# First block of an attention stage: where TensorE computes absorbed weights, biases, value tiles and the folded projection

## Chip, cores and metric

One core of one Trainium2 chip runs one program. The metric is device microseconds (us) of one execution, lower is better; the kernel before has a median of 724.17 us over 3 runs (723.96 to 729.38).

## What is computed

Two transformer layers over x of 2048 x 128 fp32, each an attention and a mixture of experts, with a layer norm before each of the four. Only the first attention matters here (8 heads, head width 128, latent width 32):

```
c_q = h @ W_DQ + b_DQ;  c_kv = h @ W_DKV + b_DKV          # h = layernorm(x), 2048 x 32 each
q = [c_q @ W_UQ + b_UQ, c_q @ W_QR + b_QR]                 # per head: 128 + 32
k = [c_kv @ W_UK + b_UK, h @ W_KR + b_KR]                  # the last 32 are shared by the heads
attn = softmax(q @ k.T / sqrt(160))
o = attn @ (c_kv @ W_UV + b_UV)
x = x + o @ W_O + b_O
```

## The kernel before

**Absorbed form.** For each head, W_UQ and W_UK (with the W_QR part) are multiplied once into a 128 x 128 matrix, the absorbed weights; with it the latents of the whole sequence (`kk`, 2048 columns) become this head's keys in latent space (`key`). Scores are then products of latent queries with `key`. The value side stays latent too (`val`, 2048 x 32): W_UV and W_O are multiplied into one matrix a head (`proj`, the folded projection), and the biases of value and output give one row (`g_b`), which is spread over 128 partitions (`g_bias`) and added to X. Heads come in two groups of four: group 0 is `absorbed(0)`, group 1 `absorbed(1)`.

**Blocks.** A block n is one head and 512 queries; there are 32. For each block TensorE makes two things. *Row products* (`rows`, `half_rows`, L1507): 128 queries against 1024 keys as two halves of 512 columns in two PSUM banks; eight of them, called chunks, make a block, and VectorE takes the maximum of each (`chunk_max`, L1087 for both halves in one instruction ahead of the first block, L1093 for one half within the blocks), then the negative maximum of all queries (`minus_max`, L1101, tile `nmx`), which SyncE's DMA puts into `q_cols` as one more row (the shift). *Scores* (`scores`, L1521): 128 keys against 512 queries, which ScalarE turns into exponentials (L651), sixteen tiles a block, in three PSUM banks (0, 1, 2). The exponentials go into the weighted sums (`weighted`, L1565, eight tiles a call). Row products run ten chunks (LEAD) ahead of the scores, so chunks 0 to 9 are made before the first block: chunks 0 to 7 belong to block 0, 8 and 9 to block 1.

**Order of the work.** Each engine has one instruction list written by hand, and semaphores between them. A block's loop has eight slots; in each TensorE makes two score tiles and the two halves of one row product. A table worked out ahead (`BANK`, `BEFORE`) gives the items of the loop the banks 3 to 6 in turn, in the order in which they are listed, and `bank_read` waits until the item that was in the bank has been read. `chunks_read(c)` waits until VectorE has read chunks 0 to c - 1.

**What stands around the change.** Ahead of the first block TensorE alternates row products with the rest of the preparation: `absorbed(1)` into bank 2 (L1470, L1471, four heads), `key_biases(1, 1)` (L1476) and the row `g_bias` (L1666) into bank 1, `queries(1, 0)` (L1461) into bank 0, and value tiles (`values`, L1464) into bank 7. Each has a reader: ScalarE and then VectorE split absorbed weights into a high and a low part (L605, L1072), VectorE reads the key biases (L1116, L1119), ScalarE copies `g_bias` (L675), and ScalarE and VectorE make `q_rows` of the query product (L600, L1066). A row product of the first chunk of a block uses that block's `q_rows`: for chunk 8 it is the query block 1. In `half_rows` this stands as

```
if h == 0 and c == 0 and j == 0:
    pe.wait_ge(s_cq, k + 1)
```

Behind chunk 9 TensorE waits for all of these readers at once before the first score tile. In the first block value tiles 12 to 15 stand in slot 1, VectorE's addition of the value bias (L1123) in slot 2, and `folded()` (L1482, 32 matmuls of the code into two banks) in slot 5, with ScalarE's two copies of it (L610) ahead of exponential 12. `weighted(0, 0)` stands in slot 6.

Of the kernel before, what the change touches and what calls it, by code (L numbers as in the profile page):

```python
# [14 lines left out]
TPB = BLK // P  # L15
# [3 lines left out]
def build_kernel(nc, d, out):  # L19

    S, D = d["L0_attn_h_t"].shape[1:]
    NT = S // P
# [10 lines left out]
    with ctx:  # L33
# [213 lines left out]
        for n in range(NBLK):  # L247
            todo = []
            for slot in range(CPB):
                for lin in row_pairs(n, slot):  # L250
                    todo += [("rows", 2 * lin), ("rows", 2 * lin + 1)]
                todo += [("keys", e) for e in key_parts(n, slot)]
                if slot == 0 and n < 2:
                    todo.append(("queries", n + 2))
                if slot == 5 and n == 0:
                    todo += [("folded", 0), ("folded", 1)]
                if slot == 1 and 4 <= n < NBLK - 2:
                    todo.append(("out", n - 4))
                if (slot == 6 and n == NBLK - 3) or (slot == 3 and n == NBLK - 2):
                    todo.append(("out", n - 3))  # L260
                if slot == 1 and n == NBLK - 2:
                    todo.append(("sums", n - 2))
                if slot == 6 and 2 <= n < NBLK - 2:
                    todo.append(("sums", n - 2))
                if slot == 6 and n == NBLK - 2:
                    todo.append(("out", n - 2))
            for item in todo:
                place_item(item, 3 + turn % 4)
                turn += 1
# [177 lines left out]
        with nc.Block() as block:  # L447
# [104 lines left out]
            def _(act):  # L552
# [50 lines left out]
                def absorbed_hi(m):  # L603
                    act.wait_ge(s_a_ps, m + 1)
                    act.copy(wa_hi[:, 4 * m:4 * (m + 1), :], ps[:, A_BANK[m], :].rearrange("p (h c) -> p h c", h=4)).then_inc(s_wah, 1)  # L605
# [67 lines left out]
                keys_hi(3, 0)  # L673
                act.wait_ge(s_b_ps, 2)
                act.copy(g_bias[:, :], ps[:, 1, 0:D]).then_inc(s_gbias, 1)  # L675
                absorbed_hi(1)
                queries_hi(1, 0)
                for n in range(NBLK):
                    for t in range(NT):
                        if t == 4 and n >= 1:  # L680
                            sums(n - 1)
                        if t == (14 if n < NBLK - 2 else 4) and n >= 2:
                            sums_out(n - 2)
                        if t == 10 and n == NBLK - 1:
                            sums_out(n - 1)
                        if t % 2 == 0 and t >= 2:
                            for e in key_parts(n, t // 2 - 1):
                                keys_hi(e, BANK["keys", e])
                        if t == 2 and n < 2:
                            queries_hi(n + 2, BANK["queries", n + 2])  # L690
                        if t == 12 and n == 0:
                            folded()
                        exponential(n, t)
                        if n == NBLK - 1 and t == 10:
                            ln0_act(act, 0, 3)
# [347 lines left out]
            def _(dve):  # L1043
# [135 lines left out]
                        dve.tensor_tensor(g_b[:, :], ps[0:1, 1, 0:D], b_o[:, :], ALU.add).then_inc(s_gb, 1)  # L1179
                minus_max(0)  # L1180
                queries_lo(1, 0)
                absorbed_lo(1)
                key_biases(1, 1)
                for lin in range(CPB, LEAD):
                    chunk_max(lin)
                for n in range(NBLK):
                    for slot in range(CPB):
                        lins = row_pairs(n, slot)
# [251 lines left out]
            def _(pe):  # L1440
# [23 lines left out]
                    return pe.matmul(ps[:, U, t * C:(t + 1) * C], hT[:, t // TPB, t % TPB * P:(t % TPB + 1) * P], w_kk[:, 0:C],  # L1464
                                     start=True, stop=True)

                def absorbed(m):
                    for h in range(4 * m, 4 * (m + 1)):
                        o = ps[:, A_BANK[m], (h % 4) * P:(h % 4 + 1) * P]
                        pe.matmul(o, ukT[:, h, :], uqT[:, h, :], start=True, stop=False)  # L1470
                        last = pe.matmul(o, qr_at[:, h, :], place[:, :], start=False, stop=True)  # L1471
                    last.then_inc(s_a_ps, 1)

                def key_biases(m, bank):
                    for h in range(4 * m, 4 * (m + 1)):
# [38 lines left out]
                def scores(n, t):  # L1514

                    g = NT * n + t
                    if t == 0:
                        pe.wait_ge(s_shift, 16 * (n + 1))
                    if g >= 3:
                        pe.wait_ge(s_exp, g - 2)  # L1520
                    pe.matmul(ps[:, g % 3, :], key[:, n // NB % KBUF, t * P:(t + 1) * P], q_cols[:, n % NB, :],  # L1521
                              start=True, stop=True).then_inc(s_sc, 1)

# [133 lines left out]
                rows(4)  # L1657
                chunks_read(4)
                rows(5)
                absorbed(1)  # L1660
                chunks_read(5)
                rows(6)
                pe.wait_ge(s_gb, 1)
                key_biases(1, 1)
                pe.wait_ge(s_const, N_ONES)
                pe.matmul(ps[:, 1, 0:D], ones_row[:, :], g_b[:, :], start=True, stop=True).then_inc(s_b_ps, 1)  # L1666
                chunks_read(6)
                rows(7)
                queries(1, 0)
                for t in range(2 * TPB):  # L1670
                    values(t)
                chunks_read(7)
                rows(8)
                chunks_read(8)
                rows(9)
                for t in range(2 * TPB, 3 * TPB):
                    values(t)
                pe.wait_ge(s_kb, 3)
                pe.wait_ge(s_gbias, 1)
                pe.wait_ge(s_cq, 2)  # L1680
                pe.wait_ge(s_wal, 2)
                for n in range(NBLK):
                    for slot in range(CPB):
                        scores(n, 2 * slot)
                        for lin in row_pairs(n, slot):
                            bank_read(("rows", 2 * lin))
                            half_rows(lin, 0)
                        scores(n, 2 * slot + 1)
                        for lin in row_pairs(n, slot):
                            bank_read(("rows", 2 * lin + 1))  # L1690
                            half_rows(lin, 1)
                        for e in key_parts(n, slot):
                            bank_read(("keys", e))
                            keys(e, BANK["keys", e])
                        if slot == 0 and n < 2:
                            bank_read(("queries", n + 2))
                            queries(n + 2, BANK["queries", n + 2])
                        if slot == 1 and n == 0:
                            for t in range(3 * TPB, NT):
                                last = values(t)  # L1700
                            last.then_inc(s_val_ps, 1)
                        if slot == 5 and n == 0:
                            bank_read(("folded", 0))
                            bank_read(("folded", 1))
                            folded()
                        if slot == 1 and 4 <= n < NBLK - 2:
                            output(n - 4)
                        if (slot == 6 and n == NBLK - 3) or (slot == 3 and n == NBLK - 2):
                            output(n - 3)
                        if slot == 6 and n == NBLK - 2:  # L1710
                            output(n - 2)
                        if slot == 6:
                            weighted(n, 0)
                        if slot == 6 and 2 <= n < NBLK - 2:
                            totals(n - 2)
                        if slot == 6 and n == NBLK - 1:
                            last_totals(0)
                            last_totals(1)
                        if slot == 1 and n >= 1:
                            weighted(n - 1, 1)  # L1720
                        if slot == 1 and n >= NBLK - 2:
                            totals(n - 2)
                        if n == NBLK - 1:
                            if slot == 2:
                                output(n - 2)
                            elif slot == 4:
                                totals(n - 1)
                                bank_read(("norm", 0))
                                ln0_pe(pe, 0, 3)
                            elif slot == 7:  # L1730
                                output(n - 1)
                                last_totals(2)
                                bank_read(("norm", 1))
                                ln0_pe(pe, 1, 4)
                                weigh(n, range(2 * NG, 3 * NG))
# [350 lines left out]
```

## Time and profile before

| | |
|---|---|
| median of 3 runs | 724.17 us |
| the profiled execution | 724.64 us, its span 722.8 us |
| TensorE busy | 703.9 us, 97% |
| VectorE busy | 582.5 us, 81% |
| ScalarE busy | 459.8 us, 64% |
| GpSimd busy | 540.0 us, 75% |
| granted TensorE clock, mean of the span | 0.998 |

PE is TensorE's matmuls, PEld its weight loads, DVE VectorE, ACT ScalarE, POOL GpSimd, SP SyncE. A row of the timeline gives the start and the duration in us, engine, line, operation, tile written and tiles read, shapes, how many instructions were merged (x2), and in brackets how long the engine had been idle just before and what ended that. One matmul of the code on plain fp32 data appears as two records, one on fp32r data as one. The end of a matmul is modelled: in an unbroken row the next one starts before it.

### The profile page before, as it was taken

The numbers are of one execution on the slowest core, as the hardware profiler recorded it, in microseconds if no ns is written. First come the engines' busy times: TensorE is split into PE (matmuls) and PEld (weight loads), VectorE is DVE, ScalarE is ACT, GpSimd is POOL, SyncE is SP. The second block draws the span as 40 slices with busy tenths as digits, with TensorE's granted clock in tenths as the row PEclk, the third lists the DMA queues.
The fourth block names the chain that finished last, engine by engine and source line by source line (L and its number), as shares of the span: only waits on it lengthen the run. The fifth ranks groups of instructions, "written<-read, shape, count | busy, mean of one in ns | idle before, by whom it ended". The sixth has DMA issues, their size and how long they took to land.

```text
span 722.8 us, 12898 instructions
## 1 busy us (share of the span) xinstructions
PE 703.9 (97%) x4488; PEld 475.8 (66%) x4488; DVE 582.5 (81%) x1213; ACT 459.8 (64%) x1069; POOL 540.0 (75%) x440
## 2 busy tenths in 40 slices
PE   8999999999999999999999999999899999999997
PEld 6665666666566566566566566566566599778885
DVE  7878888988988988888988887846977636878885
ACT  4357876776776776676776666745787822455553
POOL 6468998988998998988998997515688751446674
PEclk9999999999999999999999999999999999999999
DMA  6313666567467466467467474030000000032431
GB/s 151 92 38 67 132 124 133 96 125 136 93 128 135 90 131 133 90 130 132 89 132 132 89 142 94 1 107 16 0 2 1 1 2 1 1 88 77 145 102 30
DMA packets 38853, 61.55 MB, mean 85 GB/s; under 512 B 14456, under 2 KB 23689, under 8 KB 34948
## 3 DMA queue, kind: packets, MB, share of 16 engines
q0 software_dynamic: 11936, 46.14, 32.8%
q1 hardware_dynamic: 25572, 14.47, 7.6%
q8 instruction: 36, 0.59, 0.3%
q10 hardware_dynamic: 1280, 0.12, 0.1%
q14 instruction: 29, 0.24, 0.1%
HBM read 13.35 MB, written 1.10 MB: 20 GB/s over the span
## 4 chain that ended last, share of the span: by engine, by line
PE 74%; POOL 10%; DVE 6%; issue 6%; DMA 1%; ACT 1%; POOLq 0%; DVEq 0%
PE ps L1521 17%; PE ps L1565 16%; PE ps L1507 15%; POOL hid_lo L1039 5%; PE ps L1928 4%; PE ps L1549 4%; DVE mx L1093 2%; POOL nrm L1019 2%; PE ps L1585 2%; PE ps L1968 2%; PE ps L1970 2%; PE ps L1969 2%; POOL hid L1019 1%; PE ps L1494 1%; PE ps L1495 1%
## 5 line engine op out<-in xcount | busy, mean ns | idle before, releaser
L1093 DVE TENSOR_REDUCE mx<-ps 128x1 f32<-128x512 f32 x492 | 303.0, 683 | 52.2 <-PE ps L1507 52.0
L651 ACT ACTIVATE prob<-ps 128x512 f32<-128x512 f32 x512 | 261.7, 631 | 18.4 <-PE ps L1521 14.3
L1521 PE MATMUL ps<-q_cols,key 128*128 128x512 f32 x512 | 210.3, 414 | 0.8 <-ACT prob L651 0.4
L1507 PE MATMUL ps<-key,q_rows 128*128 128x512 f32 x512 | 203.1, 401 | 0.8 <-DVE key L1079 0.4
L1521 PEld LDWEIGHTS ps<-q_cols,key 128*128 128x128 f32 x512 | 95.4, 187 | 72.6 <-issue 34.1
L937 POOL TENSOR_TENSOR part<-prob 128x512 f32<-128x512 f32 x84 | 115.1, 1508 | 23.1 <-ACT prob L651 22.9
L1565 PE MATMUL ps<-prob,val 128*32 128x512 f32 x1024 | 123.3, 598 | 0.0
L1507 PEld LDWEIGHTS ps<-key,q_rows 128*128 128x128 f32 x512 | 95.7, 188 | 19.0 <-DVE mx L1087 1.4
L951 POOL TENSOR_TENSOR pair<-prob 128x512 f32<-128x512 f32 x60 | 87.0, 1470 | 9.1 <-ACT prob L651 8.9
L1039 POOL TENSOR_TENSOR hid_lo<-hid,hid_hi 128x512 fp32r<-128x512 f32 x44 | 61.4, 1407 | 38.8 <-ACT hid_hi L817 38.7
L937 POOL TENSOR_TENSOR w_v<-prob 128x512 f32<-128x512 f32 x40 | 55.4, 1564 | 11.5 <-ACT prob L651 11.5
L1565 PEld LDWEIGHTS ps<-prob,val 128*32 128x32 f32 x1024 | 26.7, 109 | 50.9 <-issue 46.9
L958 POOL TENSOR_TENSOR part<-part,pair 128x1024 f32<-128x1024 f32 x20 | 48.3, 2414 | 0.0
L801 ACT ACTIVATE act_g<-ps 128x512 f32<-128x512 f32 x44 | 26.3, 599 | 33.2 <-PE ps L1970 33.0
L1143 DVE SCALAR_TENSOR_TENSOR X<-ps,rden,X 128x128 f32<-128x128 f32 x128 | 36.0, 344 | 7.5 <-PE ps L1549 4.2
L769 ACT ACTIVATE pT<-ps 128x128 f32<-128x128 f32 x128 | 33.6, 278 | 10.7 <-PE ps L1905 10.7
L632 ACT COPY den_sb<-ps 128x128 f32<-128x128 f32 x31 | 8.2, 266 | 50.6 <-PE ps L1585 50.1
L1406 DVE TENSOR_TENSOR prod<-ps,act_g 128x512 f32<-128x512 f32 x44 | 30.2, 685 | 11.0 <-PE ps L1970 8.8
L624 ACT COPY u_sb<-ps 128x512 f32<-128x512 f32 x22 | 12.9, 586 | 40.1 <-PE ps L1565 40.1
L335 POOL TENSOR_SCALAR vare<-mv 128x4 f32<-128x4 f32 x12 | 4.7, 390 | 41.5 <-DVE mv L329 41.2
L1968 PE MATMUL ps<-hT_hi,w_hi 128*128 128x512 f32 x88 | 35.5, 403 | 0.0
L1970 PE MATMUL ps<-hT_lo,w_hi 128*128 128x512 f32 x88 | 34.6, 393 | 0.0
(292 smaller groups left out, 1248.4 us busy)
## 6 DMA issues: line engine op xcount, KB each, us to landing
part<-prob POOLq DMA_DIRECT2D x20, 1024.0 KB, 7.2
w_v<-prob POOLq DMA_DIRECT2D x10, 1024.0 KB, 7.6
part<-part POOLq DMA_DIRECT2D x19, 512.0 KB, 6.5
w_v<-w_v POOLq DMA_DIRECT2D x9, 512.0 KB, 7.3
g_all<-g_rows SPq DMA_DIRECT2D x9, 256.0 KB, 3.3
g_all<-g_rows SPq DMA_DIRECT2D x6, 224.0 KB, 2.9
X<-in_L_attn_h_t_dram SPq DMA_DIRECT2D x4, 256.0 KB, 4.2
out_dram<-X SPq DMA_DIRECT2D x4, 256.0 KB, 2.7
```

The source lines that it names most:

```text
L651: act.activation(prob[:, g % RING, :], ps[:, g % 3, :], ACT.Exp, scale=SCALE).then_inc(s_exp, 1)
L937: pool.tensor_tensor(part[n % 3][:, g, :], tiles(n, 2 * g, 1)[:, 0, :], tiles(n, 2 * g + 1, 1)[:, 0, :], ALU.add).then_inc(s_sum, 1)
L951: pool.tensor_tensor(pair[:, j, :], tiles(n, t, 1)[:, 0, :], tiles(n, t + 1, 1)[:, 0, :], ALU.add).then_inc(s_pair, 1)
L958: pool.tensor_tensor(p, p, pair[:, :, :], ALU.add).then_inc(s_sum, 1)
L1039: pool.tensor_tensor(hid_lo[:, n % 4, :], hid[:, n % 2, :], hid_hi[:, n % 4, :].bitcast(F32), ALU.subtract).then_inc(s_hlo, 1)
L1093: dve.tensor_reduce(mx[:, n % 2, c % TPB, at:at + 1], ps[:, BANK["rows", 2 * lin + j], :], AX.X, ALU.max).then_inc(s_mrd, 1)
L1143: last = dve.scalar_tensor_tensor(out=xt, in0=ps[:, BANK["out", n], i * P:(i + 1) * P], scalar=rden[:, n % 2, i:i + 1], in1=xt, op0=ALU.mu ...
L1507: pe.matmul(ps[:, BANK["rows", 2 * lin + j], :], q_rows[:, k, i * P:(i + 1) * P], key[:, h % KBUF, c0:c0 + BLK], start=True, stop=True).th ...
L1521: pe.matmul(ps[:, g % 3, :], key[:, n // NB % KBUF, t * P:(t + 1) * P], q_cols[:, n % NB, :], start=True, stop=True).then_inc(s_sc, 1)
L1565: last = pe.matmul(ps[C * x:C * (x + 1), U, :], val[:, t, :], prob[:, (NT * n + t) % RING, :], start=(t < NG), stop=(t >= NT - NG))
L1968: pe.matmul(out_ps, w[0], x_hi, start=start, stop=False)
L1970: return pe.matmul(out_ps, w[0], x_lo, start=False, stop=stop)
```

## The change

Six things are moved; no arithmetic is added or removed.

- `absorbed(1)` is cut by head: head 4 between row products 5 and 6, head 5 between 6 and 7, heads 6 and 7 behind 8.
- `key_biases(1, 1)` goes from behind row product 6 to behind 8, and now waits for `g_bias` to be copied (its bank). The `g_bias` row stays behind row product 6.
- Value tiles 0 to 7 (behind `queries(1, 0)`) and 8 to 11 (behind row product 9) become tiles 0 to 3 behind row product 9, 4 to 9 in slot 1 and 10 to 15 in slot 2 of the first block.
- `folded()` goes from slot 5 to slot 6, behind `weighted(0, 0)`; ScalarE's copies go from ahead of exponential 12 to ahead of 14.
- The common wait ahead of the first block is divided: score tile 0 waits for `queries(1, 0)` to be read, tile 1 for the key biases, tile 2 for the low part of the absorbed weights.
- ScalarE takes query block 1 ahead of the absorbed weights; VectorE takes chunk 8 ahead of the low part and the key biases, and chunk 9 behind them.

```diff
-                if slot == 5 and n == 0:
+                if slot == 6 and n == 0:
                     todo += [("folded", 0), ("folded", 1)]
...
+                queries_hi(1, 0)
                 absorbed_hi(1)
-                queries_hi(1, 0)
...
-                        if t == 12 and n == 0:
+                        if t == 14 and n == 0:
                             folded()
...
                 queries_lo(1, 0)
+                chunk_max(CPB)
                 absorbed_lo(1)
                 key_biases(1, 1)
-                for lin in range(CPB, LEAD):
-                    chunk_max(lin)
+                chunk_max(CPB + 1)
...
-                def absorbed(m):
-                    for h in range(4 * m, 4 * (m + 1)):
+                def absorbed(m, first=0, count=4):
+                    for h in range(4 * m + first, 4 * m + first + count):
...
-                    last.then_inc(s_a_ps, 1)
+                    if first + count == 4:
+                        last.then_inc(s_a_ps, 1)
...
                     if g >= 3:
                         pe.wait_ge(s_exp, g - 2)
+                    elif g == 0:
+                        pe.wait_ge(s_cq, 2)
+                    elif g == 1:
+                        pe.wait_ge(s_kb, 3)
+                    else:
+                        pe.wait_ge(s_wal, 2)
...
                 rows(5)
-                absorbed(1)
+                absorbed(1, 0, 1)
                 chunks_read(5)
                 rows(6)
                 pe.wait_ge(s_gb, 1)
-                key_biases(1, 1)
                 pe.wait_ge(s_const, N_ONES)
                 pe.matmul(ps[:, 1, 0:D], ones_row[:, :], g_b[:, :], start=True, stop=True).then_inc(s_b_ps, 1)
+                absorbed(1, 1, 1)
                 chunks_read(6)
                 rows(7)
                 queries(1, 0)
-                for t in range(2 * TPB):
-                    values(t)
                 chunks_read(7)
                 rows(8)
+                absorbed(1, 2, 2)
+                pe.wait_ge(s_gbias, 1)
+                key_biases(1, 1)
                 chunks_read(8)
                 rows(9)
-                for t in range(2 * TPB, 3 * TPB):
+                for t in range(TPB):
                     values(t)
-                pe.wait_ge(s_kb, 3)
-                pe.wait_ge(s_gbias, 1)
-                pe.wait_ge(s_cq, 2)
-                pe.wait_ge(s_wal, 2)
...
-                        if slot == 1 and n == 0:
-                            for t in range(3 * TPB, NT):
+                        if slot in (1, 2) and n == 0:
+                            for t in range(6 * slot - 2, 6 * slot + 4):
                                 last = values(t)
-                            last.then_inc(s_val_ps, 1)
-                        if slot == 5 and n == 0:
-                            bank_read(("folded", 0))
-                            bank_read(("folded", 1))
-                            folded()
+                            if slot == 2:
+                                last.then_inc(s_val_ps, 1)
...
                         if slot == 6:
                             weighted(n, 0)
+                        if slot == 6 and n == 0:
+                            bank_read(("folded", 0))
+                            bank_read(("folded", 1))
+                            folded()
```

TensorE's list of before, from row product 7 (the first two rows) to the first score tile. L1461 is the query product, L1464 the value tiles, L1521 a score tile, and the brackets name the semaphores waited for (s_mrd: chunks read, s_cq: query rows ready):

```order
L1507 MATMUL ps<-key,q_rows 128x512 [waits s_mrd]
L1507 MATMUL ps<-key,q_rows 128x512
L1461 MATMUL ps<-hT,w_cq 128x512
L1464 MATMUL ps<-w_kk,hT 128x32 x8
L1507 MATMUL ps<-key,q_rows 128x512 [waits s_cq,s_mrd]
L1507 MATMUL ps<-key,q_rows 128x512
L1507 MATMUL ps<-key,q_rows 128x512 [waits s_mrd]
L1507 MATMUL ps<-key,q_rows 128x512
L1464 MATMUL ps<-w_kk,hT 128x32 x4
L1521 MATMUL ps<-q_cols,key 128x512 [waits s_wal,s_cq,s_shift,s_gbias,s_kb]
```

The same place of the changed list, from row product 7 to the first half of row product 9. A row product is L1508 here, L1470 and L1471 are one head of the absorbed weights, L1477 the key biases:

```order
L1508 MATMUL ps<-key,q_rows 128x512 [waits s_mrd]
L1508 MATMUL ps<-key,q_rows 128x512
L1461 MATMUL ps<-hT,w_cq 128x512
L1508 MATMUL ps<-key,q_rows 128x512 [waits s_cq,s_mrd]
L1508 MATMUL ps<-key,q_rows 128x512
L1470 MATMUL ps<-uqT,ukT 128x128
L1471 MATMUL ps<-place,qr_at 128x128
L1470 MATMUL ps<-uqT,ukT 128x128
L1471 MATMUL ps<-place,qr_at 128x128
L1477 MATMUL ps<-ukb,uqT 128x1 [waits s_gbias]
L1477 MATMUL ps<-ukb,uqT 128x1 x3
L1508 MATMUL ps<-key,q_rows 128x512 [waits s_mrd]
```

The eight value tiles between the query product and row product 8 are gone; two heads and the key biases now stand behind row product 8.

VectorE's list at the same place, as a difference (L1101 is the negative maximum of block 0, L1087 the maximum of a chunk, L1072 the low part of the absorbed weights):

```order
 L1101 TENSOR_REDUCE nmx<-mx 128x4
 L1066 SCALAR_TENSOR_TENSOR q_rows<-ps,unit,q_rows 128x512
+L1087 TENSOR_REDUCE mx<-ps 128x2
 L1072 TENSOR_TENSOR wa_lo<-ps,wa_hi 128x512
 L1116 TENSOR_SCALAR kcol<-ps,unit 128x4
 L1119 TENSOR_SCALAR kcol_m<-kcol,unit 128x4
-L1087 TENSOR_REDUCE mx<-ps 128x2 x2
+L1087 TENSOR_REDUCE mx<-ps 128x2
```

Of the two maxima behind the key biases one (chunk 8) is now ahead of the low part.

## Rows read from the trace of the kernel before

**Rows 1.** The page: busy time by engine, and the chain by engine

```profile
PE 703.9 (97%) x4488; PEld 475.8 (66%) x4488; DVE 582.5 (81%) x1213; ACT 459.8 (64%) x1069; POOL 540.0 (75%) x440
...
PE 74%; POOL 10%; DVE 6%; issue 6%; DMA 1%; ACT 1%; POOLq 0%; DVEq 0%
```

**Rows 2.** Windows: length, busy us (x count) of PE, PEld, DVE, ACT, POOL; granted clock, DMA

```profile
120.00:140.00 20.00, 20.00 (x131) 12.46 (x130) 17.60 (x36) 14.05 (x29) 17.07 (x14) 1.00 0.74 142
```

**Rows 3.** Timeline, 26 to 42 us: what leads to the first block

```profile
28.81 0.73 PE L1507 MATMUL ps<-key,q_rows 128*128 128x512 f32 x2 [0.34 <-DVE mx L1087]
...
30.00 1.20 DVE L1087 TENSOR_REDUCE mx<-ps 128x2 f32<-128x1024 f32 x1
...
31.89 1.23 DVE L1087 TENSOR_REDUCE mx<-ps 128x2 f32<-128x1024 f32 x1 [0.69 <-PE ps L1507]
...
33.18 0.59 ACT L605 CAST wa_hi<-ps 128x512 fp32r<-128x512 f32 x1
...
33.49 1.02 PE L1461 MATMUL ps<-hT,w_cq 128*128 128x512 f32 x2
...
33.76 1.22 DVE L1087 TENSOR_REDUCE mx<-ps 128x2 f32<-128x1024 f32 x1 [0.64 <-PE ps L1507]
...
34.35 1.87 PE L1464 MATMUL ps<-w_kk,hT 128*128 128x32 f32 x16
...
35.36 0.75 DVE L1066 SCALAR_TENSOR_TENSOR q_rows<-ps,unit,q_rows 128x512 fp32r<-128x512 f32 x1 [0.17 <-ACT q_rows L600]
36.02 0.68 DVE L1072 TENSOR_TENSOR wa_lo<-ps,wa_hi 128x512 fp32r<-128x512 f32 x1
...
36.26 1.17 PE L1507 MATMUL ps<-key,q_rows 128*128 128x512 f32 x4
...
37.06 2.36 DVE L1087 TENSOR_REDUCE mx<-ps 128x2 f32<-128x1024 f32 x2
...
38.07 0.47 PE L1521 MATMUL ps<-q_cols,key 128*128 128x512 f32 x1
...
39.47 0.50 PE L1494 MATMUL ps<-kk,wa_hi 128*128 128x512 f32 x1 [0.17 <-DVE mx L1087]
...
41.59 0.40 PE L1507 MATMUL ps<-key,q_rows 128*128 128x512 f32 x1
```

**Rows 4.** The chain that ended last, 28 to 41 us: start, us, what

```profile
29.54 0.22 PE ps L1470 x2
...
31.33 0.46 PE ps L1507 x2
31.79 0.79 PE ps L1476 x8
32.57 0.41 PE ps L1666 x2
```

**Rows 5.** Timeline, 42 to 60 us: the first block

```profile
43.55 0.50 PE L1507 MATMUL ps<-key,q_rows 128*128 128x512 f32 x1 [0.45 <-DVE key L1079]
...
44.21 0.50 PE L1507 MATMUL ps<-key,q_rows 128*128 128x512 f32 x1
...
45.95 3.67 DVE L1093 TENSOR_REDUCE mx<-ps 128x1 f32<-128x512 f32 x6
...
48.58 1.95 PE L1482 MATMUL ps<-w_o,uvT 128*32 128x128 f32 x64 [0.79 <-DVE mx L1093]
...
57.74 1.92 PE L1565 MATMUL ps<-prob,val 128*32 128x512 f32 x16
```

**Rows 6.** The chain that ended last, 47 to 60 us

```profile
50.53 0.43 PE ps L1521
50.96 0.23 PE ps L1507
...
51.66 1.85 PE ps L1565 x16
```

**Rows 7.** Windows, 22 to 24 us, columns as in rows 2

```profile
22.00:24.00 2.00, 1.04 (x4) 0.30 (x2) 2.00 (x4) 1.11 (x2) 1.51 (x3) 1.00 0.90 296
```

## Prediction

> **What bounds the kernel now.** I read the page first: TensorE is busy 97% of the span and has 74% of the chain that ended last [rows 1]. The windows say where: in 120 to 140 us TensorE is busy 20.00 of 20.00 us, VectorE 17.60 and ScalarE 14.05 [rows 2]. From the second block on the stage runs at the pace of TensorE's own list, so whatever the stretch up to there gains or loses passes to the end unchanged. No engine's work inside the steady blocks is altered. The question is therefore only how much earlier TensorE enters them. As the mark I take the second half of block 0's weighted sum, at 57.74 us [rows 5].
>
> The timeline ahead of it shows who waits. Between row product 5 (28.81 us) and the first score tile (38.07) VectorE's reductions are the pace, but with two gaps, 0.69 us ahead of chunk 6 and 0.64 ahead of chunk 7, both ended by TensorE's row products [rows 3]: TensorE computes four heads, key biases and the bias row between them. In the first block it is TensorE that waits: for `key` ahead of row product 12, and 0.79 us by its row ahead of the folded projection [rows 5].
>
> **Unit prices.** One head is two such pairs as the 0.22 of L1470, 0.44 us; a row product of two halves is 0.46, key biases 0.79, the bias row 0.41 [rows 4]. The query product takes 34.35 - 33.49 = 0.86 of TensorE and is ready after 1.02; eight value tiles take 1.87, so 0.23 each; a matmul that had to wait shows 0.50 (39.47 us) where an unbroken one shows 0.40 (41.59 us) [rows 3], so I count 0.11 more after a wait. Reductions of a whole chunk follow each other every 1.16 us (2.36 for two, less 1.20 for a single one) [rows 3].
>
> **Step 1, heads split between row products (a gain).** Row product 5 starts at 28.81 in both. Behind it, 0.57 later, now stands one head instead of four: 29.38 to 29.82. Row product 6 waits for chunk 4 to be read, just before the reduction at 30.00, so it starts near 29.95 and ends at 30.5; bias row 0.41 and head 5 0.44 lead to 31.35, row product 7 to 31.8. With 0.05 for changing between unlike matmuls the query product starts at 31.85, against 33.49 before: 1.64 us earlier. VectorE meanwhile runs chunks 5, 6 and 7 without a gap from 30.00, 31.16 and 32.32 to 33.5.
>
> **Step 2, the eight value tiles no longer cover the query rows (a loss, and the main point).** Row product 8 is the first chunk of block 1 and needs `q_rows` of that block; its wait on s_cq stands in both lists. From the start of the query product to the end of VectorE's subtraction it is 35.36 + 0.75 - 33.49 = 2.62 us [rows 3]. Before, 0.86 of product and 1.87 of value tiles lay over that, 2.73 together, and row product 8 started at 36.26 without a wait. Now only the 0.86 lies over it: the rows are ready at 31.85 + 2.62 = 34.47 (VectorE is free at about 33.6, so it adds nothing), TensorE has nothing from 32.71 to 34.5 and stands for 1.8 us. Everything stands behind that wait in TensorE's list: two heads, key biases, row product 9, four value tiles, the first scores.
>
> From 34.5: row product 8 with 0.11, 0.57; heads 6 and 7, 0.88, to 35.95; key biases to 36.75; row product 9 to 37.2; four value tiles 0.94, to 38.15. The first score tile starts at 38.15 against 38.07: no gain at all there.
>
> **Step 3, up to the first key product of the loop.** That product (39.47 before) needs chunk 9 read. The heads are complete at 36.1; ScalarE's copy 0.59 [rows 3] gives 36.75; VectorE's low part and the two bias operations take 37.06 - 36.02 = 1.04 [rows 3], to 37.8; chunk 9 is read at 39.0. TensorE arrives after two scores and row product 10, four times 0.23, at 38.15 + 0.92 = 39.07. So both meet, and the key product starts 0.4 us earlier than 39.47. It, the query product behind it, and the subtractions on VectorE that release row product 12 keep their distances, so 0.4 is what row product 12 gains. Slot 1 holds two value tiles more than before (0.46); they lie in TensorE's wait ahead of row product 12, whose row shows 0.45 of idle [rows 5].
>
> **Step 4, from row product 12's second half to the mark.** Before: 57.74 - 44.21 = 13.53 us [rows 5]. The time that TensorE stood in it: 44.21 + 0.34 + three slots of 0.92 is 47.31, and the folded projection starts at 48.58, so 1.27. Now the six value tiles of slot 2 come in: + 1.40. The folded projection stands behind row product 16 and the weighted sum, so its banks have long been read: - 1.27. A score behind the folded projection or a weighted sum costs 0.43 instead of 0.23 [rows 6]; the two now stand together, so one such change goes: - 0.20 (the trace does not show a folded projection behind a weighted sum; its change may cost between 0 and the same 0.20, and I take 0.1). Sum: - 1.27 + 1.40 - 0.20 + 0.1 = 0.0.
>
> Hidden and priced at nothing: ScalarE's copies of the folded projection (their banks are wanted again only in block 1's slot 0, 1.4 us later); VectorE's addition of the value bias, which waits for the last tile and would be missed only by the weighted sum at 49 us; the shift of block 1, whose negative maximum falls near 50 us with its DMA 2 us, where scores of block 1 start at 54; the bias row's earlier landing, which lets GpSimd begin 1.6 us sooner on X with nothing waiting for it. Cover gone: if the maximum were 2 us later, TensorE would wait for the DMA one to one.
>
> **The sum.** - 0.4 + 0.0 = - 0.4 us. The profiled execution would go from 724.64 to 724.2; it lies 0.5 above the median of the runs, 724.17, so the median goes to 723.8. A measurement of this kernel tells about 1% (7 us) from no change, so this is no change.
>
> **Bounds.** The wait at row product 8 is 1.5 to 2.1 us (the three hand-overs, each 0.1 more or less). Three waits or changes more between heads and row products cost 0 to 0.11 each. If TensorE, not VectorE, were late at the key product, 0 of the 0.4 is left; if step 4 gains its 0.2, 0.6. Own range of this case: 723.3 to 724.3.
>
> **Rivals.**
>
> *The order does what it is laid out for.* If row product 8 did not stand, VectorE would run unbroken: chunk 7 to 33.5, query rows to 34.4, chunk 8 to 35.55, the 1.04, chunk 9 to 37.8, 1.6 earlier than before: 722.5 us. For it: the gaps at chunks 6 and 7 do close. Against it: the wait on s_cq in the list. 11%.
>
> *Slower: VectorE becomes late for row product 16.* Its half banks need chunk 14 read. VectorE can start on the value bias only at 45.6, behind the last tile; then every 0.61 (3.67 for six) [rows 5] a half: chunk 14 read at 48.1 and 48.7. TensorE comes at 48.55 and 49.0, so the margin is 0.3 to 0.4. It decides from there on: to be slower than before VectorE must be 0.7 late. With the whole 0.7 of each reduction instead of the overlapped 0.61, and a start held up by the late slot, 1.2 late costs 0.9: 724.7 us. 16%.
>
> *The clock falls in the new wait.* In 22 to 24 us TensorE was busy 1.04 of 2.00 and the granted clock was 1.00, that is 2.4 GHz [rows 7]. Should it fall to 1.2 GHz, the 3.5 us of work from row product 8 to the first score take twice that: 727.3 us. 3%. The Trainium skill (TensorE: Matmul & The Clock Gate, the section on the HAM clock gate) says that an idle stretch throttles the array to half its clock; the trace shows no such fall at an idle 0.96 of 2 us, and no longer stand is in it before the first block.
>
> **How the numbers follow.** My case has 70%. The time is its own, 723.8; the range takes in most of the slower rival and the upper part of what lies between mine and the fast one: 722.7 to 725.0. No case reaches 7 us either way: 1% faster, 98% within, 1% slower.
>
> **What would show it.** In the changed profile: VectorE's reductions of chunks 5, 6 and 7 without a gap; the query product near 31.9; then an idle of TensorE of about 1.8 us, ended by VectorE's `q_rows`, ahead of row product 8 near 34.5; the first score near 38.1 and the first key product near 39.1; the folded projection behind the weighted sum with no wait; the mark near 57.3. I am wrong if that idle is under 1 us, if the mark lies under 56.5 or above 58, or if TensorE waits for VectorE at row products 15 or 16.

## The result, and the profile after

The changed kernel is slower: 729.3 us median of 20 runs (727.29 to 731.53) against 724.62 for the kernel before, measured beside it (20 runs: 19 of 723.49 to 729.38, and one of 1393.94 that stands apart); ratio 1.0059, 95% interval 1.0049 to 1.0070. I had forecast 723.8, in a range of 722.7 to 725.0.

The profiled execution of the changed kernel took 727.29 us, span 725.5, against 724.64 and 722.8 before. TensorE's busy time hardly moved ([rows 1]: 703.9), so the loss is idle time. The page of the changed kernel, the busy line and two of the costliest groups (a score tile is L1528 here, a row product L1508):

```profile
PE 702.5 (97%) x4488; PEld 475.5 (66%) x4488; DVE 582.6 (80%) x1213; ACT 460.1 (63%) x1069; POOL 540.7 (75%) x440
...
L1528 PE MATMUL ps<-q_cols,key 128*128 128x512 f32 x512 | 210.2, 413 | 3.8 <-DMA q_cols<-nmx 3.2
L1508 PE MATMUL ps<-key,q_rows 128*128 128x512 f32 x512 | 202.9, 400 | 2.1 <-DVE q_rows L1066 1.7
```

Two idle times are new: 1.7 us ended by VectorE's `q_rows`, which I had forecast, and 3.2 us ended by the DMA `q_cols<-nmx`, which I had not. First the lead-in, the timeline of the changed kernel, to be laid beside [rows 3]:

```profile
28.52 0.73 PE L1508 MATMUL ps<-key,q_rows 128*128 128x512 f32 x2 [0.35 <-DVE mx L1087]
...
29.72 3.52 DVE L1087 TENSOR_REDUCE mx<-ps 128x2 f32<-128x1024 f32 x3
...
31.75 1.02 PE L1461 MATMUL ps<-hT,w_cq 128*128 128x512 f32 x2
...
34.51 0.69 PE L1508 MATMUL ps<-key,q_rows 128*128 128x512 f32 x2 [1.75 <-DVE q_rows L1066]
...
38.05 1.21 DVE L1087 TENSOR_REDUCE mx<-ps 128x2 f32<-128x1024 f32 x1
38.10 0.48 PE L1528 MATMUL ps<-q_cols,key 128*128 128x512 f32 x1
...
39.32 0.50 PE L1495 MATMUL ps<-kk,wa_hi 128*128 128x512 f32 x1
```

VectorE's reductions of chunks 5 to 7 run without a gap (one row of three), the query product starts at 31.75, TensorE stands 1.75 us, and the first score starts at 38.10. The walk through the lists was right to 0.2 us in these positions. Now the first block, the timeline at its end:

```profile
44.41 1.42 PE L1464 MATMUL ps<-w_kk,hT 128*128 128x32 f32 x12
...
46.48 3.67 DVE L1093 TENSOR_REDUCE mx<-ps 128x1 f32<-128x512 f32 x6
...
49.64 1.11 POOL L943 DMA_DIRECT2D part<-prob  x1 [0.61 <-ACT prob L651]
50.18 0.17 DVE L1101 TENSOR_REDUCE nmx<-mx 128x4 fp32r<-128x16 f32 x1
...
57.40 0.50 PE L1528 MATMUL ps<-q_cols,key 128*128 128x512 f32 x1 [3.08 <-DMA q_cols<-nmx]
...
60.78 1.92 PE L1572 MATMUL ps<-prob,val 128*32 128x512 f32 x16
```

and the chain that ended last over the same place (start, us, what):

```profile
50.18 0.18 DVE nmx L1101
50.36 0.02 issue
50.38 6.98 DMA q_cols<-nmx
57.36 0.04 issue
57.40 0.50 PE ps L1528
```

The maximum of block 1 is written at 50.18 and its small DMA, 2 KB, is issued at 50.38, 0.74 us behind GpSimd's first accumulating DMA of 1 MB (49.64). It lands 6.98 us later. In the kernel before the two were issued together:

```profile
49.66 0.17 DVE L1101 TENSOR_REDUCE nmx<-mx 128x4 fp32r<-128x16 f32 x1
49.79 1.11 POOL L943 DMA_DIRECT2D part<-prob  x1 [0.61 <-POOL part L937]
49.85 0.50 SPq L508 DMA_DIRECT2D q_cols<-nmx  x1
```

and there the small one landed in 1.9 us, which is also the median of the 32 such DMAs in either trace. Of the 32, the longest took 2.7 us before and this one, 7.0, in the changed kernel. From row product 5 to my mark, the second half of block 0's weighted sum, the kernel before takes 57.74 - 28.81 = 28.93 us, the changed one 60.78 - 28.52 = 32.26: 3.3 us more, of which the stand is 3.1.

### The profile page after: what moved, and what is told of

Its sections match the earlier page's. It is cut to its first block, busy times and chain, and to the rows that moved or that the text cites. A ratio compares the mean times of both kernels' runs of the same rounds, so it can differ in the third digit from the quotient of the medians.

```text
span 725.5 us, 12898 instructions
## 1 busy us (share of the span) xinstructions
PE 702.5 (97%) x4488; PEld 475.5 (66%) x4488; DVE 582.6 (80%) x1213; ACT 460.1 (63%) x1069; POOL 540.7 (75%) x440
## 4 chain that ended last, share of the span: by engine, by line
PE 73%; POOL 10%; DVE 7%; issue 7%; DMA 2%; ACT 1%; POOLq 0%; DVEq 0%
PE ps L1528 17%; PE ps L1572 16%; PE ps L1508 15%; POOL hid_lo L1039 5%; PE ps L1933 4%; PE ps L1556 4%; DVE mx L1093 2%; POOL nrm L1019 2%; PE ps L1592 2%; DMA q_cols<-nmx 2%; PE ps L1973 2%; PE ps L1975 2%; PE ps L1974 1%; POOL hid L1019 1%; PE ps L1495 1%
## 5 line engine op out<-in xcount | busy, mean ns | idle before, releaser
L1528 PE MATMUL ps<-q_cols,key 128*128 128x512 f32 x512 | 210.2, 413 | 3.8 <-DMA q_cols<-nmx 3.2
L1508 PE MATMUL ps<-key,q_rows 128*128 128x512 f32 x512 | 202.9, 400 | 2.1 <-DVE q_rows L1066 1.7
L1528 PEld LDWEIGHTS ps<-q_cols,key 128*128 128x128 f32 x512 | 95.4, 187 | 74.2 <-issue 33.2
L1508 PEld LDWEIGHTS ps<-key,q_rows 128*128 128x128 f32 x512 | 95.7, 188 | 20.2 <-issue 2.5
L1416 DVE TENSOR_TENSOR hid<-g_all,prod 128x512 f32<-128x512 f32 x26 | 30.6, 1176 | 5.0 <-POOL hid_lo L1039 4.4
```

The costliest lines, as they stand in the source:

```text
L1508: pe.matmul(ps[:, BANK["rows", 2 * lin + j], :], q_rows[:, k, i * P:(i + 1) * P], key[:, h % KBUF, c0:c0 + BLK], start=True, stop=True).th ...
```

## The experiments

Two theories stood at first. Theory Q: the small DMA queues behind the 1 MB one, and the rest is the stand that follows. Rival S: VectorE's later maximum or the folded projection's new place costs by itself. A third question came with the numbers: the profiled execution is 2 us under the median of the runs, so something costs more in most of them (theory C, the clock).

**e1, the 1 MB DMA behind the maximum.** The changed kernel with

```diff
                     ready(n, 3 * NG - 1)
+                    if n == 0:
+                        pool.wait_ge(s_sel, 2)
```

> The changed kernel, with one wait more: GpSimd issues the first accumulating DMA (1 MB, part<-prob, L943, block 0) only once the negative maximum of block 1 is written. It then stands at or behind the small DMA q_cols<-nmx instead of 0.74 us ahead of it. Theory Q (the small DMA queues behind the 1 MB one on the same 16 DMA engines): it lands 1.9 us after its issue instead of 7.0, TensorE's stand of 3.1 us ahead of block 1's first score is gone, the span falls by 3.1 from 725.5 to about 722.4, time near 724. Rival S (the shift is late because VectorE writes the maximum 0.5 us later and the folded projection is behind the weighted sum): the stand stays, 727 to 729. Rival C (the rest of the loss is the clock that falls in an idle TensorE): if the stand goes, the mean clock of the runs returns to that of before as well, and with it the 2 us by which most runs lie above the profiled one.

Measured: 725.04 us (10 runs) against 725.81 (21 runs of the kernel before), ratio 0.9992, interval 0.9971 to 1.0013. The order of the two DMAs in its trace, and the mark:

```profile
50.49 0.50 SPq L508 DMA_DIRECT2D q_cols<-nmx  x1
51.06 1.11 POOL L945 DMA_DIRECT2D part<-prob  x1 [1.88 <-DVE nmx L1103]
...
57.55 1.92 PE L1574 MATMUL ps<-prob,val 128*32 128x512 f32 x16
```

The small DMA is issued at the same time as in the changed kernel, only first; it lands in 1.9 us, no score waits for it, and the loss is gone. The mean clock is under 0.998 in 5 of these 10 runs, as in 12 of the 21 of the kernel before, so what lay above the first profile goes with the stand, as rival C expected. With e2, which makes the opposite step, this settles the 3 us: it is the order of two DMAs. What is left of the change is 57.55 - 28.65 = 28.90 from row product 5 to the mark, 0.03 less than before.

**e2, the kernel before with the small DMA late.** SyncE waits for exponential 12 of block 0 ahead of block 1's shift:

```diff
                     sp.wait_ge(s_sel, n + 1)
+                    if n == 1:
+                        sp.wait_ge(s_exp, 13)
```

> The kernel before, with one wait more: SyncE issues the DMA q_cols<-nmx of block 1 only behind exponential 12 of block 0, about 51.6 us instead of 49.85, so behind GpSimd's 1 MB DMA (49.8). Nothing else moves. Its plain 1.9 us would land it at 53.5, and block 1's first score is due at 54.6: hidden. Theory Q: it lands when the 1 MB is through, near 57, TensorE stands 2 to 3 us, time 727 to 730. Rival S: no stand, 724.6, the same as before.

Measured: 729.04 us (4 runs), ratio 1.0046, interval 1.0028 to 1.0064. Its timeline:

```profile
51.59 0.50 SPq L510 DMA_DIRECT2D q_cols<-nmx  x1
...
57.27 0.80 PE L1523 MATMUL ps<-q_cols,key 128*128 128x512 f32 x1 [2.79 <-DMA q_cols<-nmx]
```

So one DMA issued 1.7 us later, which would have been hidden with room to spare, makes the kernel before as slow as the changed one. It lands 5.6 us after its issue, when the 1 MB is through (issued at 49.63, landed 7.4 later). The clock of this execution falls too, in the windows around and behind the stand; one of them (columns as in [rows 2], the granted clock third from the end):

```profile
57.00:59.00 2.00, 1.73 (x4) 1.44 (x5) 0.47 (x1) 0.64 (x2) 0.00 (x0) 0.50 0.00 0
```

**e3, the value tiles back.** The changed kernel with tiles 0 to 7 behind the query product, 8 to 11 behind row product 9, 12 to 15 in slot 1:

```diff
                 queries(1, 0)
+                for t in range(2 * TPB):
+                    values(t)
...
-                for t in range(TPB):
+                for t in range(2 * TPB, 3 * TPB):
                     values(t)
...
-                        if slot in (1, 2) and n == 0:
-                            for t in range(6 * slot - 2, 6 * slot + 4):
+                        if slot == 1 and n == 0:
+                            for t in range(3 * TPB, NT):
                                 last = values(t)
-                            if slot == 2:
-                                last.then_inc(s_val_ps, 1)
+                            last.then_inc(s_val_ps, 1)
```

> The changed kernel with the value tiles where they were before (0 to 7 behind the query product, 8 to 11 behind row product 9, 12 to 15 in slot 1). The wait for the query rows ahead of row product 8 (1.75 us) is covered by the eight tiles again, and VectorE no longer waits 0.56 us for tile 15, so the maximum of block 1 comes near 49.5 instead of 50.2, at or ahead of GpSimd's 1 MB DMA (49.6). Theory Q: landing 1.9 us, no stand, time 723.5 to 724.5. Rival S: the folded projection behind the weighted sum is what costs, 727 or more.

Measured: 724.98 us (10 runs), ratio 0.9990, interval 0.9970 to 1.0009: no difference that can be told, and 0.5 us above the expected range. The trace is clearer: the maximum at 49.66, the 1 MB at 49.79 and the small DMA at 49.85, as in the kernel before, landing in 1.9 us. TensorE does not stand ahead of row product 8 (it starts at 34.65 behind eight value tiles), and the mark stands at

```profile
56.81 1.92 PE L1572 MATMUL ps<-prob,val 128*32 128x512 f32 x16
```

56.81 - 28.66 = 28.15 from row product 5, 0.78 less than before and 0.75 less than in e1, so the value tiles in their new places cost 0.75 even without the DMA. Where the 0.78 is gained can be read too. The first key product starts at 39.46 here, 10.80 behind row product 5, exactly as in the changed kernel and 0.14 later than before; row product 8 starts 5.99 behind it, also as in the changed kernel. So covering the stand makes nothing earlier up to there, and the heads split by itself has brought nothing by then. The whole gain lies behind the key product (17.35 us to the mark against 18.27), where the folded projection's new place is the difference to the kernel before; that it alone brings it was not tested. The maximum was at 49.66 and not at 49.5 as expected, at the edge.

**e4, the folded projection back in slot 5.**

```diff
-                if slot == 6 and n == 0:
+                if slot == 5 and n == 0:
                     todo += [("folded", 0), ("folded", 1)]
...
-                        if t == 14 and n == 0:
+                        if t == 12 and n == 0:
                             folded()
```

and TensorE's `folded()` with its two `bank_read` calls likewise.

> The changed kernel with the folded projection back in slot 5 (and its copies ahead of exponential 12). Theory Q: the maximum is still written near 50.2, behind the 1 MB DMA at 49.6, so the stand of 3 us and the loss stay: 727 to 730. Rival S (the folded projection in the new place delays what leads to block 1): the loss goes, about 724.

Measured: 728.64 us (6 runs), ratio 1.0039, interval 1.0016 to 1.0062. The maximum at 50.22, the 1 MB at 49.71, the small DMA at 50.41, landing in 7.4 us, and the stand is there:

```profile
49.13 1.95 PE L1483 MATMUL ps<-w_o,uvT 128*32 128x128 f32 x64 [0.44 <-DVE mx L1093]
57.89 0.50 PE L1528 MATMUL ps<-q_cols,key 128*128 128x512 f32 x1 [2.69 <-DMA q_cols<-nmx]
```

Rival S falls for the folded projection.

**e8, VectorE's value addition late.** What makes the maximum late? The changed kernel with that addition behind the maximum:

```diff
-                        if slot == 2 and n == 0:
-                            values()
                         if CPB * (n + 2) - 1 in lins:
                             minus_max(n + 1)
+                        if slot == 5 and n == 0:
+                            values()
```

> The changed kernel with VectorE's addition of the value bias moved from slot 2 to slot 5, behind the maximum of block 1; TensorE's list is untouched. What makes the maximum 0.5 us late? Theory T (TensorE's six value tiles in slot 2 delay row product 13, whose halves VectorE needs at 46.4): VectorE has nothing to do in the freed time, the maximum comes near 50.1, GpSimd's DMA at 49.6 stays ahead, stand of 3 us, 728 to 730. Rival V (VectorE's addition, which waits 0.56 us for tile 15 and takes 0.6): the maximum comes at 49.0 to 49.4, ahead of GpSimd's DMA; landing 1.9 us, no stand, 724 to 725.

Measured: 728.1 us (9 runs), ratio 1.0037, interval 1.0009 to 1.0064. VectorE only waits longer, for TensorE:

```profile
46.59 3.68 DVE L1093 TENSOR_REDUCE mx<-ps 128x1 f32<-128x512 f32 x6 [1.12 <-PE ps L1508]
49.82 1.11 POOL L943 DMA_DIRECT2D part<-prob  x1 [0.61 <-ACT prob L651]
50.30 0.17 DVE L1101 TENSOR_REDUCE nmx<-mx 128x4 fp32r<-128x16 f32 x1
...
51.12 1.92 PE L1572 MATMUL ps<-prob,val 128*32 128x512 f32 x16 [1.36 <-DVE val L1123]
...
57.16 0.50 PE L1528 MATMUL ps<-q_cols,key 128*128 128x512 f32 x1 [1.23 <-DMA q_cols<-nmx]
```

It is TensorE's six value tiles in slot 2 that hold back row product 13, and with it the six half reductions and the maximum. Rival V falls. The small DMA is issued at 50.50, 0.68 us behind the large one, and lands in 6.6. The stand ahead of block 1 is 1.23 us and not the 3 expected, because the weighted sum has stood 1.36 us earlier, for the addition that was moved.

**e5, the changed kernel again.**

> The changed kernel itself once more, for another profile. The placement of block 1's first score does not change: the DMA q_cols<-nmx lands 7 us after its issue and TensorE stands about 3 us. Open is what lifts most of its executions (729 to 731) over the profiled one (727.3). Theory C: the stand makes the clock fall in most executions, and costs 1 to 3 us more; a profile of such an execution shows a granted clock well under 1.00 in the windows behind 57 us. Rival N: the clock behind the stand is 1.00 there too, and the scatter is the same as that of the kernel before.

Measured: 729.62 us (7 runs), ratio 1.0060, interval 1.0035 to 1.0085. This profile (span 727.5) shows what the first one lacked. Windows of 2 us around and behind the stand (columns as in [rows 2], the granted clock third from the end):

```profile
55.00:57.00 2.00, 0.00 (x0) 0.00 (x0) 0.31 (x1) 0.00 (x0) 1.26 (x1) 1.00 0.71 136
57.00:59.00 2.00, 1.42 (x4) 1.17 (x5) 0.50 (x1) 0.67 (x2) 0.00 (x0) 0.76 0.00 0
59.00:61.00 2.00, 2.00 (x6) 1.20 (x5) 0.89 (x2) 1.30 (x2) 1.27 (x1) 0.50 0.00 0
61.00:63.00 2.00, 2.00 (x10) 0.88 (x12) 0.79 (x2) 1.24 (x3) 0.00 (x0) 0.89 0.03 8
63.00:65.00 2.00, 2.00 (x18) 0.74 (x11) 1.82 (x3) 0.95 (x3) 0.12 (x1) 1.00 0.00 0
```

After a stand of 3.13 us, with no matmul at all in 55 to 57, TensorE works at 1.2 GHz (0.50) and then again at 2.4. A score that takes 0.40 shows 0.63 in this trace, and matmuls start every 0.43 us instead of every 0.23:

```profile
57.58 0.50 PE L1528 MATMUL ps<-q_cols,key 128*128 128x512 f32 x1 [3.13 <-DMA q_cols<-nmx]
57.92 0.54 PE L1508 MATMUL ps<-key,q_rows 128*128 128x512 f32 x1
58.26 0.63 PE L1528 MATMUL ps<-q_cols,key 128*128 128x512 f32 x1
58.69 0.63 PE L1508 MATMUL ps<-key,q_rows 128*128 128x512 f32 x1
```

The mark stands at 62.58, where the first profile, whose windows all show 1.00 there, has 60.78: 1.8 us, of which 0.14 is a later start, so 1.7 for the clock. Theory C holds for this execution.

**e7, the stand filled.** The changed kernel with useless matmuls while TensorE would stand:

```diff
                     for slot in range(CPB):
+                        if n == 1 and slot == 0:
+                            pe.wait_ge(s_exp, 14)
+                            spin(13, 1)
                         scores(n, 2 * slot)
```

> The changed kernel with 13 matmuls of no use (128x128, 2.9 us) on TensorE while it would stand for the late shift of block 1; the stand itself stays as long. Theory C (idle TensorE loses its clock): the runs lose their upper part, mean clock 0.998 and more, median near 727.5 instead of 729. Rival N: nothing changes, 729.

Measured: 728.32 us (11 runs), ratio 1.0045, interval 1.0024 to 1.0067. The same windows show 1.00 throughout, for instance

```profile
57.00:59.00 2.00, 1.43 (x8) 1.09 (x8) 0.22 (x1) 0.46 (x1) 0.00 (x0) 1.00 0.03 8
```

and 2 of its 11 executions have a mean clock under 0.998, where the changed kernel has 23 of 27 (e5 and the 20 runs of the result together). Its median lies 1.3 us under e5's, run beside it, though work was added. It is above the 727.5 expected: the first score starts at 58.00 in its profile instead of 57.58, 7.4 us behind the issue of the small DMA instead of 7.1, and with the last filling matmuls just ahead of it.

**e6, mended, with row product 9 forward.** The changed kernel with e1's wait, and

```diff
                 queries(1, 0)
+                for t in range(2 * TPB):
+                    values(t)
                 chunks_read(7)
                 rows(8)
+                chunks_read(8)
+                rows(9)
                 absorbed(1, 2, 2)
                 pe.wait_ge(s_gbias, 1)
                 key_biases(1, 1)
-                chunks_read(8)
-                rows(9)
-                for t in range(TPB):
-                    values(t)
...
-                            for t in range(6 * slot - 2, 6 * slot + 4):
+                            for t in (range(8, 14) if slot == 1 else range(14, NT)):
...
                 chunk_max(CPB)
+                chunk_max(CPB + 1)
+                key_biases(1, 1)
                 absorbed_lo(1)
-                key_biases(1, 1)
-                chunk_max(CPB + 1)
```

> The changed kernel mended at three places: value tiles 0 to 7 stand behind the query product again and cover the wait for the query rows, 8 to 13 in slot 1, 14 and 15 in slot 2; row product 9 stands ahead of heads 6 and 7 and chunk 9 is reduced ahead of the key biases; GpSimd's first 1 MB DMA waits for the maximum of block 1. Theory Q and the walk through the lists: no stand ahead of row product 8, the first key product near 38.4 instead of 39.3 to 39.5, the second half of block 0's weighted sum near 56.0 instead of 57.74, no stand at block 1, time 1.5 us under the kernel before run beside it. Rival (VectorE is the bound of the first block whatever TensorE does): the mark stays at 57 or later, no gain that can be measured.

Measured: 723.57 us (12 runs) against 725.89 (25 runs), ratio 0.9968, interval 0.9951 to 0.9985. It is faster than the kernel before, by some 2 us, more than the 1.5 expected, and 6 us under e5, the changed kernel run beside it. Its timeline, first key product and mark:

```profile
38.49 0.39 PE L1497 MATMUL ps<-kk,wa_hi 128*128 128x512 f32 x1
...
55.75 1.92 PE L1574 MATMUL ps<-prob,val 128*32 128x512 f32 x16
```

From row product 5 (28.60) to the mark it takes 27.15 us, 1.78 less than before. The rival, VectorE as the bound whatever TensorE does, falls. What each of its changes brings was not taken apart.

**e9, e6 without the added wait.**

> e6 without GpSimd's added wait: the order of the lists alone decides which DMA is first. The maximum of block 1 is written at 48.6 to 48.8, exponential 11 is done near 48.4 and GpSimd's last sum near 48.15 + 0.6, so its 1 MB DMA is issued at 48.7 to 48.8, within 0.1 us of the small one. Theory Q: within so little the small one still lands in 1.9 us, as in the kernel before (49.79 against 49.85); time as e6, some 1.5 us under the kernel before. Rival (any issue ahead of it is enough): landing near 7 us, and with it a stand of some 3 us.

Measured: 724.25 us (10 runs) against 725.82 (19 runs), ratio 0.9974, interval 0.9951 to 0.9996. The two issues are 0.05 us apart, 1 MB first (48.93, 48.98), and the small one lands in 1.9 us; the mark is again 27.15 behind row product 5 (55.94 - 28.79). So the order of the lists is enough, but its margin is slim: the large DMA issued 0.05 us ahead does no harm, issued 0.7 us ahead (e4, e5, e7, e8 and the changed kernel) it holds the small one until the end. Where between them it turns was not tried. The packets give an estimate: in each of the eleven profiles here the first packet of the 1 MB starts 1.67 to 1.68 us behind its issue, and where the small DMA is not held its first packet starts 1.15 to 1.17 behind its own, its last 0.2 later. By this it should turn at a lag of 0.3 to 0.5 us.

## Why the prediction was wrong

**Step 1 (heads split) and step 2 (the wait for the query rows)** held. The query product came at 31.75 (31.85 forecast) and the stand was 1.75 us (1.8). What it costs was less plain than the forecast has it: with the stand covered (e3) row product 8 and the first key product start no earlier, and what is lost by moving the eight tiles is their own time in the first block, 0.75 us. Counted from row product 5, which the profile has 0.29 earlier than before for a reason that lies ahead of the change, all is some 0.2 to 0.3 later than I had it: the query product 3.23 behind it instead of 3.04, row product 8 5.99 instead of 5.69.

**Step 3** was over-sized. The first key product starts 39.32 - 28.52 = 10.80 behind row product 5, before 39.47 - 28.81 = 10.66: a loss of 0.14 where I had a gain of 0.4. Half of it is the 0.3 above; the other is the low part and key biases, 38.05 - 36.75 = 1.30 instead of 1.04. Why the same three instructions take 0.26 longer no run shows.

**Step 4** was right in its sum. In e1, where the late shift is taken away, the stretch from the key product to the mark is 57.55 - 39.44 = 18.11 against 18.27 before. Without the DMA the change would have been -0.03 instead of -0.4: no change, as forecast. In part that sum was luck. In the same stretch e3, without the tiles in slot 2, gains 18.27 - 17.35 = 0.92 where my other terms gave 1.37, and the tiles cost 18.11 - 17.35 = 0.76 where I had 1.40: two terms, each too large, that cancel.

**The step that failed** is the sentence in step 4 that the shift is hidden, "whose negative maximum falls near 50 us with its DMA 2 us". The maximum did fall at 50.2; the DMA took 6.98 us and not 2, and TensorE stood 3.1 us for it where I had priced the wait at nothing. I took a duration from rows in which the small DMA is issued ahead of or with the large one, and did not ask what the change does to their order. The trace of before held the warning: the issues stand 0.06 us apart. The six value tiles of slot 2 move the maximum by 0.5 us (0.7 counted from row product 5 against e3, 21.66 against 21.00), while GpSimd's DMA, which waits for exponential 11 and GpSimd's own sums, stays at its place (21.12 against 21.13). A slack of 2 us at the wait said nothing, since the price behind it jumps from 1.9 to 7.0. I named the condition ("if the maximum were 2 us later") and had the wrong quantity in it. The mark at 60.78 is above the 58 that I had named as a sign of being wrong. Nor was it right that a measurement tells only about 7 us from no change: the interval of the 4.7 us measured is 1.0049 to 1.0070.

**The rivals.** The slower rival was VectorE late for row product 16: TensorE waits nowhere at row products 15 and 16 in the profile. The clock rival looked at the wrong stand. The 1.75 us ahead of row product 8 did not bring the clock down in either profile of the changed kernel; the 3.1 us ahead of block 1 did in e5, but not in the first profile, and of two stands of 2.8 and 2.7 us that of e2 did and that of e4 did not (1.00 in all windows of 2 us from 55 to 63). The forecast's sentence that no longer stand is in the trace of before overlooks the 1.58 us ahead of its first matmul. The loss of clock explains most of the way from the 3 us of the first profile to the 4.7 of the medians. The Trainium skill (TensorE: Matmul & The Clock Gate, the HAM clock gate) says that an idle array is throttled to half its clock. The trace of e5 agrees (0.50 in 59 to 61), while the first profile, of the same program with the same stand, shows no fall at all. The page also says that the point at which the clock changes varies from run to run, but of the rise at the start of a kernel; that the fall varies is what these two profiles show. The kernel before loses clock too in many runs (15 of the 25 beside e5 to e7 have a mean under 0.998), and such a loss can lie far behind the change: e1's profile, at 729.2 us, has 0.55 in 490 to 500 us and no stand at block 1. This scatter is larger than what e1 and e3 change, so the positions in the trace carry those two verdicts.

**How the small DMA is held.** The packets of the two queues show it in part. Each of the two DMAs has 144 packets, 9 for each of 16 engines. These are the packets that start in a stretch, by the view of the DMA queues; q0 is GpSimd's 1 MB, q1 SyncE's 2 KB:

| profile | stretch, us | q0 | q1 |
|---|---|---|---|
| kernel before | 49 to 51.4 | 0 | 144 |
| changed kernel | 49 to 53 | 48 | 0 |
| changed kernel | 53 to 56 | 80 | 80 |
| changed kernel | 56 to 57 | 16 | 64 |
| e2 | 52.5 to 56 | 96 | 0 |
| e2 | 56 to 56.5 | 16 | 139 |

In the kernel before the small one is done before the large one's first packet. In the changed kernel, while the large one runs, the two queues start as many packets each from 53 us on, and the small one's last 64 follow when only 16 of the large one are left. In e2, issued later, the small one starts none in 52.5 to 56 us, though its first was due at 52.8.

The Trainium skill (DMA: Bandwidth & Descriptors, Queues, rings and completion order) says that an engine takes its queues in turn and empties a whole packet, of several descriptors, from one before it goes to the next. The changed kernel's trace agrees as to the turns; e2's does not show them. Whether a packet of the profile is a packet or a descriptor of that page, no run shows.

**Open.** Why the small DMA's first packet starts 2.8 us behind its issue in the changed kernel instead of 1.2, when three rows of the large one's packets have started, and why in e2 it gets no turn at all. No run has a large DMA that does not accumulate, or one of another size, so it is not shown which of these properties matters.

## What to carry to other kernels

A wait that ends on a small DMA is priced by what is in the DMA engines when it is issued: look for large transfers issued ahead of it, also from another engine (0.7 and 2 us ahead did harm here), and check after every reordering that the small one is still first. A wait on the producer's semaphore ahead of the large issue (e1) makes that order firm, and cost nothing that could be measured here. When work is moved behind a product, ask what it had been covering: here eight value tiles lay over the 1.8 us for which TensorE then stood, and took their own time elsewhere. And count a stand of TensorE of 3 us with the loss of clock that may follow it.

## What I had not expected of the hardware

A 2 KB DMA took 6.6 to 7.4 us instead of 1.9 when it was issued 0.7 us behind a 1 MB accumulating one (the changed kernel, e4, e5, e7, e8), and 5.6 when it was issued 2 us behind it (e2). With the large one 0.05 us ahead it still took 1.9 (e9): the large one's first packet starts only 1.7 us behind its issue. The granted clock fell to 0.50 after a stand of 3.1 us in one profile (e5) and stayed at 1.00 after the same stand in another of the same program.
